# A feed-forward stage written out without loops: the down blocks of one token tile between the gate/up units of the next

## The reference

```
x = x + cross_attention(layernorm(x), ctx_2048)            # 512 wide, output projection wo
x = x + causal_attention(layernorm(x))                     # 16 heads of 128, rope, biases
x = x + ffn(layernorm(x))
ffn(x): gate, up = x @ W_gu.T   (W_gu: 2816 x 512, fp4 codes times a scale per 128 inputs)
        h = silu(gate) * up     (1408 wide)
        y = h @ W_down.T        (W_down: 512 x 1408, fp4 codes times scales)
        return y / sqrt(mean(y*y) + 1e-6)
```

## Time and profile before

| | us |
|---|---|
| median of 3 runs | 1392.92 (1392.2 to 1392.96) |
| the profiled execution, its own time | 1399.19 |
| span of its instructions | 1397.4 |
| TensorE busy in the span | 1344.6 |
| VectorE busy | 1006.3 |
| ScalarE busy | 507.1 |
| GpSimd busy | 375.9 |

### The profile page before, as it was taken

The page is one execution under the profiler, slowest core; times in us unless marked ns, Lnnn a source line. Parts: engine busy times, 40 slices in busy tenths (PEclk is TensorE's granted clock), DMA queues, the critical chain, the costliest instruction groups (busy, mean ns, idle before and its releaser), DMA issues. The chain is left out here.

```text
span 1397.4 us, 24040 instructions
## 1 busy us (share of the span) xinstructions
PE 1344.6 (96%) x9220; PEld 776.4 (56%) x9220; DVE 1006.3 (72%) x2309; ACT 507.1 (36%) x1249; POOL 375.9 (27%) x302
## 2 busy tenths in 40 slices
PE   8999999967999999999999999999899999999998
PEld 6666666534666666666666666654344434343433
DVE  6444444247888888888888887838899696969693
ACT  3222222222343333433343334320001665748281
POOL 0000000003222222222222222203033482919192
PEclk9999999989999999999999999999999999999999
DMA  8555555522101111111201021376841000000000
GB/s 333 211 197 199 202 192 189 214 83 87 31 31 31 44 45 50 31 31 61 61 31 31 16 61 31 91 190 193 187 162 61 1 1 30 0 30 0 30 1 30
DMA packets 36927, 122.47 MB, mean 88 GB/s; under 512 B 4313, under 2 KB 4953, under 8 KB 28121
## 3 DMA queue, kind: packets, MB, share of 16 engines
q1 hardware_dynamic: 36552, 118.19, 25.4%
q10 hardware_dynamic: 272, 2.88, 0.9%
HBM read 95.89 MB, written 25.17 MB: 87 GB/s over the span
## 5 line engine op out<-in xcount | busy, mean ns | idle before, releaser
L871 POOL TENSOR_TENSOR hd_rotated<-hd_products 64x512 f32<-64x512 f32 x32 | 40.3, 1259 | 741.0 <-DVE hd_products L1123 741.0
L191 PE MATMUL psum<-hd_xt_hi,hqk_hi 128*128 128x512 f16 x512 | 194.6, 380 | 1.6 <-DVE hd_xt_lo L1097 1.6
L192 PE MATMUL psum<-hd_xt_lo,hqk_hi 128*128 128x512 f16 x512 | 194.3, 379 | 0.0
L193 PE MATMUL psum<-hd_xt_hi,hqk_lo 128*128 128x512 f16 x512 | 194.3, 379 | 0.0
L1480 POOL TENSOR_TENSOR ff_part<-ff_part 128x512 f32<-128x512 f32 x88 | 127.8, 1468 | 103.9 <-DVE ff_part L1607 103.5
L191 PE MATMUL psum<-hd_wv_hi,hd_xt_hi 128*128 128x256 f16 x512 | 140.3, 274 | 4.2 <-DVE hd_wv_lo L1102 4.2
L1509 PE MATMUL psum<-ff_xt_hi,gu 128*128 128x512 f16 x352 | 133.9, 380 | 9.0 <-DVE w_rows L1645 3.3
L192 PE MATMUL psum<-hd_wv_lo,hd_xt_hi 128*128 128x256 f16 x512 | 140.4, 274 | 0.0
L193 PE MATMUL psum<-hd_wv_hi,hd_xt_lo 128*128 128x256 f16 x512 | 140.3, 274 | 0.0
L1510 PE MATMUL psum<-ff_xt_lo,gu 128*128 128x512 f16 x352 | 133.4, 379 | 0.0
L1607 DVE SCALAR_TENSOR_TENSOR ff_part<-psum,gu_scale,ff_part 128x512 f32<-128x512 f32 x176 | 119.8, 738 | 6.3 <-ACT ff_part L1557 3.6
(11 more groups left out here) (181 smaller groups left out, 3007.1 us busy)
## 6 DMA issues: line engine op xcount, KB each, us to landing
xa_kv_t<-in_ctx_t_dram SPq DMA_DIRECT2D x16, 1024.0 KB, 5.7
xa_kv<-in_ctx_dram SPq DMA_DIRECT2D x16, 1024.0 KB, 4.8
w_rows<-in_head_weights_dram SPq DMA_DIRECT2D x12, 1024.0 KB, 8.0
z_scratch<-hd_z_hi SPq DMA_DIRECT2D x32, 256.0 KB, 2.6
z_scratch<-hd_z_lo SPq DMA_DIRECT2D x32, 256.0 KB, 3.3
w_rows<-z_scratch SPq DMA_DIRECT2D x8, 1024.0 KB, 8.9
hqk_lo<-z_scratch SPq DMA_DIRECT2D x8, 1024.0 KB, 8.4
xn<-in_x_dram SPq DMA_DIRECT2D x8, 512.0 KB, 3.9
```

What stands on the lines that cost most here:

```text
L191: pe.matmul(out, lh, rh, start=(first and i == 0), stop=False)
L192: pe.matmul(out, lh, rl, start=False, stop=False)
L193: last = pe.matmul(out, ll, rh, start=False, stop=(final and i == k - 1))
```

## The change

The feed-forward phase is written out for all tiles. For tile 0 the 22 units run as before on eight banks. Then, for each t of 0 to 2, TensorE takes three down jobs of tile t, the transposes of tile t+1, six more jobs, and then the 22 units of tile t+1, with the other 35 jobs spread behind them: `beside` cuts the 35 jobs in 44 pieces, two pieces behind each whole unit (about 1.6 jobs). The last tile's 44 jobs run alone at the end. Groups and transposes use six banks in turn (6, 7, 0, 1, 2, 3), down products banks 4 and 5. ScalarE, after squaring, also copies the down product out of its bank into `results`, in all tiles but the last; the last step `finish` on VectorE then reads it from there. `h_hi`, `h_lo` and `results` are doubled. VectorE's layernorm is cut in pieces (`side_work`) put behind units: in tile 0 only the four `scale_block`s of tile 1, since the statistics of tile 1 are taken in `merge_phase` after add 13; in tiles 1 and 2 two block statistics behind units 0 and 2, small steps behind 4 and 6, `scale_block` behind 8, 10, 12, 14. In tiles 2 and 3 the roots of tile t-2 are behind units 5 and 7 and `finish` behind 9, 11, 13, 15. `second_halves` of the next tile come before the last `gated`. The four small transposes are gone, and the first unit waits for each `xt_lo` part alone. In `merge_phase` the load of `x1` of tile 1 moves from `heads_phase` to behind the codes of group 1, that of tile 3 to behind the next `z` load.

```diff
...
                 sp.dma_start(early.codes, codes_of(gu_codes, 0)).then_inc(early_sems.codes_loaded, 16)
-                for t in range(2):
-                    sp.dma_start(early.x2[:, t * TT:(t + 1) * TT, :], rows_of(t * TILE)).then_inc(early_sems.x1_loaded, 16)
+                sp.dma_start(early.x2[:, 0:TT, :], rows_of(0)).then_inc(early_sems.x1_loaded, 16)
...
-        x1_loaded, x1_ready = {t: sem(f"x1_{t}_loaded") for t in range(2, NT)}, sem("x1_ready")
+        x1_loaded, x1_ready = {t: sem(f"x1_{t}_loaded") for t in range(1, NT)}, sem("x1_ready")
...
+            load_x1(1)
             for t in range(1, NT - 1):
                 sp.wait_ge(z_used[1], t)
                 load_z(t, 1)
                 if t == 2:
+                    load_x1(3)
                     load_down()
                 if t == NT - 2:
                     sp.wait_ge(z_stored, 16 * (HEADS_SMALL + 2 * NT * PAIRS))
...
                 load_z(t + 1, 0)
                 if t == 1:
                     load_x1(2)
-                    load_x1(3)
...
-                    pool.wait_ge(early_sems.x1_loaded, 32)
-                if b % TT == 0 and b >= 2 * TT:
+                    pool.wait_ge(early_sems.x1_loaded, 16)
+                if b % TT == 0 and b >= TT:
...
+                if b == NT * TT - 3:
+                    dve.wait_ge(added, 2 * TT)
+                    layernorm(dve, 1, x2[:, TT:2 * TT, :], xn, stat, ln_step, xn_ready, parts=(1, 2, 3, 4))
...
+        FIRST, SECOND = 3, 9
+        jobs = [(0, b) for b in range(SECOND)] + [(1, b) for b in range(3)] + [(0, b) for b in range(SECOND, FB)] + \
+            [(1, b) for b in range(3, FB)] + [(i, b) for i in (2, 3) for b in range(FB)]
+        beside = [jobs[SECOND:][n * (len(jobs) - SECOND) // (2 * UNITS):(n + 1) * (len(jobs) - SECOND) // (2 * UNITS)] for n in range(2 * UNITS)]
+        def unit_after(i):
+            return next(n for n in range(2 * UNITS) if (i, FB - 1) in beside[n]) // 2
+        ROUND, RESULTS = (6, 7, 0, 1, 2, 3), (4, 5)
+        tile_0 = [("x", 0, k) for k in range(KD)] + [("p", 0, u, g) for u in range(UNITS) for g in range(KD)]
+        in_order = []
+        for t in range(1, NT):
+            in_order += [("x", t, k) for k in range(KD)] + [("p", t, u, g) for u in range(UNITS) for g in range(KD)]
+        placed = [(unit, n % 8) for n, unit in enumerate(tile_0)] + [(unit, ROUND[n % len(ROUND)]) for n, unit in enumerate(in_order)]
+        placed += [(("y", t, i), RESULTS[i % 2]) for t in range(NT - 1) for i in range(TT)]
+        placed += [(("y", NT - 1, i), bank) for i, bank in enumerate((4, 6, 7, 0))]
+        banks = Banks(nc, ctx, "ff", placed, [])
...
+            for t in range(NT - 1):
+                sp.wait_ge(finished, TT * (t + 1))
+                store(t, 0, TT)
...
+            def gate_up(t, u, g):
+                first = u % 2 * FF + u // 2 * P
+                unit = ("p", t, u, g)
+                if u == 0:
+                    banks.wait_moved(pe, None, ("x", t, g))
+                banks.wait_room(pe, None, unit)
+                pe.matmul(psum_of(unit), gu[:, g, first:first + P], xt_hi[:, g, :], start=True, stop=False)
+                banks.fills(pe.matmul(psum_of(unit), gu[:, g, first:first + P], xt_lo[:, g, :], start=False, stop=True), None, unit)
+            def down(t, i, b):
+                unit = ("y", t, i)
+                h_hi, h_lo = h_pairs[t % 2]
+                if b == 0:
+                    banks.wait_room(pe, None, unit)
+                if i == 0:
+                    pe.wait_ge(h_lo_done, t * FB + b + 1)
+                last = three_passes(pe, psum_of(unit), [(h_hi[:, b, block_of(i)], h_lo[:, b, block_of(i)])],
+                                    [(down_hi[:, b, :], down_lo[:, b, :])], first=(b == 0), final=(b == FB - 1))
+                if b == FB - 1:
+                    banks.fills(last, None, unit)
+            turn_xn(0)
+            for u in range(UNITS):
+                for g in range(KD):
+                    gate_up(0, u, g)
+            for t in range(NT - 1):
+                for i, b in jobs[0:FIRST]:
+                    down(t, i, b)
+                turn_xn(t + 1)
+                for i, b in jobs[FIRST:SECOND]:
+                    down(t, i, b)
                 for u in range(UNITS):
...
                     for g in range(KD):
...
+                        gate_up(t + 1, u, g)
+                    for i, b in beside[2 * u] + beside[2 * u + 1]:
+                        down(t, i, b)
+            for i, b in jobs:
+                down(NT - 1, i, b)
...
+            def square(t, i):
+                unit = ("y", t, i)
                 banks.wait_filled(act, None, unit)
...
+                if t * TT + i:
+                    act.wait_ge(squares_done, t * TT + i)
+                act.activation(junk[:, :], psum_of(unit), ACT.Square, accum_out=squares[:, t % 2, i:i + 1]).then_inc(squares_done, 1)
+                if t < NT - 1:
+                    if t >= 2:
+                        act.wait_ge(out_stored[t % 2], 16)
+                    banks.moves(act.activation(results[t % 2][:, i, :], psum_of(unit), ACT.Copy), None, unit)
...
+                        hidden_hi(t, b - 2)
+                    if b == FB and t < NT - 1:
+                        first_halves(t + 1)
+                    for i in range(TT - 1):
+                        if t and unit_after(i) in (2 * b - 1, 2 * b):
+                            square(t - 1, i)
+                if t:
+                    square(t - 1, TT - 1)
+            for i in range(TT):
+                square(NT - 1, i)
...
+                dve.tensor_scalar(to, from_, stat["meanvar"][:, i, 0:1], stat["y"][:, i:i + 1], ALU.subtract, ALU.mult).then_inc(xn_ready, 1)
...
+            def root_start(t, first, end):
+                at = slice(first, end)
+                dve.wait_ge(squares_done, t * TT + end)
+                done(dve.tensor_scalar(rms["var"][:, at], squares[:, t % 2, at], 1.0 / D, RMS_EPS, ALU.mult, ALU.add))
+                inverse_root(dve, {k: v[:, at] for k, v in rms.items()}, done, rounds=1)
+            def root_end(first, end):
+                inverse_root(dve, {k: v[:, first:end] for k, v in rms.items()}, done, seed=False, rounds=2)
+            def finish(t, i):
+                to = results[t % 2][:, i, :]
+                from_ = to
+                if t < NT - 1:
+                    banks.wait_moved(dve, None, ("y", t, i))
+                else:
+                    dve.wait_ge(out_stored[t % 2], 16)
+                    from_ = psum_of(("y", t, i))
+                dve.scalar_tensor_tensor(to, from_, rms["y"][:, i:i + 1], x2[:, t * TT + i, :], ALU.mult, ALU.add).then_inc(finished, 1)
+            def side_work(t, u):
+                if t == 0:
+                    if u in (4, 8, 12, 16):
+                        scale_block(1, u // 4 - 1)
+                    return
+                if t < NT - 1:
+                    if u in (0, 2, 4, 6):
+                        statistics(t + 1, (u // 2 + 1,))
+                    if u in (8, 10, 12, 14):
+                        scale_block(t + 1, u // 2 - 4)
+                if t >= 2:
+                    if u == 5:
+                        root_start(t - 2, 0, TT)
+                    if u == 7:
+                        root_end(0, TT)
+                    if u in (9, 11, 13, 15):
+                        finish(t - 2, (u - 9) // 2)
+            second_halves(0)
+            for t in range(NT):
                 for b in range(FB + 1):
...
+                    for u in (2 * b, 2 * b + 1) if b < FB else ():
+                        scale_and_add(t, u)
+                        side_work(t, u)
+                    if b == FB and t < NT - 1:
+                        second_halves(t + 1)
                     if b:
...
+                        gated(t, b - 1)
+            for t, first, end in ((NT - 2, 0, TT), (NT - 1, 0, 2), (NT - 1, 2, 3), (NT - 1, 3, 4)):
+                root_start(t, first, end)
+                root_end(first, end)
+                for i in range(first, end):
+                    finish(t, i)
...
         flat = hqk_lo[:, :, :].rearrange("p a n -> p (a n)")
...
+        h_pairs = (halves_in(flat, flat[:, FB * TILE:]), halves_in(*(w[:, :, :].rearrange("p a n -> p (a n)") for w in (wo_hi, wo_lo))))
+        results = tuple(w_rows[:, i, :].rearrange("p (b d) -> p b d", d=D) for i in range(2))
+        ffn_phase(nc, psum, ident, early.x2, xn, stat, gu, gu_scale, down_hi, down_lo, h_pairs, results, out.rearrange("b s d -> (b s) d"))
```

More of the change, by code:

```diff
@@ L1525, in tile @@
-                for blocks in (range(FB - 2), range(FB - 2, FB)):
-                    down(0, blocks)
-                    down(1, blocks)
-                for i in range(2, TT):
-                    if i == TT - 1 and not last_tile:
-                        turn_xn(t, t + 1)
-                    down(i, range(FB))
-            with nc.tensor.Fori(0, NT - 1) as t:
-                tile(t, False)
-            tile(NT - 1, True)
```

(32 more changed lines are left out.)

205 lines of the change are left out of this document (71 added, 134 removed).

## The result

| | before | after |
|---|---|---|
| median of five runs, us | 1392.96 (1392.2 to 1394.24) | 1384.74 (1380.16 to 1388.15) |
| ratio | | 0.9921, interval 0.9892 to 0.9951 |
| profiled execution, its own time, us | 1399.19 | 1385.5 |
| span, us | 1397.4 | 1383.7 |
| first transposes of the feed-forward phase to the end, us | 303.2 | 291.0 |

A forecast was written before the change was run, and what follows sets the result against it. The feed-forward phase was taken as bound in turn by VectorE with GpSimd, and by TensorE. Gains of 1.9 (start) and 21.1 us (stalls), less 9.1 kept or new, net 13.9: 1392.9 to 1379.0, range 1372.0 to 1387.0.

The forecast's parts named there:

- the forecast case: Whole kernel: median between 1374.5 and 1384 us, chance 0.58.
- Start: Start of the feed-forward phase: first matmul 1.9 us earlier, waits for the next low halves give 0.5 back.
- Units of tile 0: Tile 0's 22 units: 4.3 us of stall kept, scale blocks half hidden; 2.9 if hidden fully, 5.7 in the open.
- Passages: Between tiles: jobs and transposes cover hidden block 8 and low halves; 0.8 us for three passages and the last stretch.
- Tiles 1 and 3: Units of these tiles: VectorE's side work stalls TensorE 0.5 us at most in tile 1, nothing in tile 3.
- Tile 2: First four blocks of tile 2: VectorE 27.0 us against TensorE's 22.0, banks worth some 2; 3.0 us of stall.
- The last step from SBUF and ScalarE's copies: `finish` with both inputs in SBUF takes 1.1 us (bounds 0.68 and 1.47); ScalarE's twelve copies are hidden by TensorE.
- Merge phase: Statistics of tile 1 hidden in VectorE's waits; moved `x1` loads worth 0, between 1.0 us gained and 1.5 lost.
- the step from the span to the median: Whole kernel: median of runs lies 6.3 us below the profiled execution, so 1385.3 profiled and 1379.0 median.
- the signs named: Profile after: last matmul near 1376.6, first gate/up 1096.3, tile 0 units 42 us, tile 2 waits, `gated` median 0.7 to 1.3.
- A: Tiles 1 to 3: VectorE bounds, small two-input steps wait 0.4 to 0.8 us each; 1382.5 to 1392, chance 0.20.
- B: Tiles 1 to 3: every small step waits a whole 1.28 us GpSimd instruction; slower than before, 1410, chance 0.04.

The follow-up runs named there:

- The short sum: Changed kernel with GpSimd's sum over 8 of 512 columns, output of no use: phase 281.0 us, median 1376.19.
- the early blocks: Changed kernel with tile 0's four scale blocks moved from behind units 4, 8, 12, 16 to behind units 0 to 3: phase 288.9 us, median 1382.48.
- The two runs on the loads: Changed kernel with the `x1` loads at their old places, median 1385.42 against 1385.33; kernel before with only those loads moved, ratio 0.9988.
- both moves: Changed kernel with roots and last steps of tiles 2 and 3 later and tile 0's scale blocks behind units 0 to 3: medians 1377.34 and 1378.92.
- the first group: Changed kernel run again, unedited, beside 17 runs of the kernel before: 1385.33 against 1396.66 us, ratio 0.9933 (0.9910 to 0.9957).
- the two where z came first: Changed kernel with roots, last steps and scale blocks moved, plus ScalarE's code loads of groups 2 and 3 waiting for z: medians 1379.05 and 1372.59.

## Why the prediction was right

The range, 1372 to 1387, holds the median of 1384.74; the forecast of 1379.0 is 5.7 us lower, and the median lies just above the forecast case (1374.5 to 1384). The sum was nearer in the profiled execution (1385.3 said, 1385.5 measured). Point by point:

*Start.* Said 1.9 gained and 0.5 given back. The first matmul is 2.0 us earlier after the transposes, and the next three groups come 0.15 us late each, 0.5 in sum. Right.

*Units of tile 0.* Said 4.3 us of stall, between 2.9 and 5.7. Measured from first matmul to first down job, 1094.78 to 1138.75, 44.0 us, less 38.0 and the 0.5 of the start: 5.5. **The term was mis-sized.** I had taken a scale block as 0.68 us, half hidden. Three of the four took 1.5 us, because they wait for GpSimd, each for a low half just begun. The short sum shows that GpSimd is the cause, the early blocks that the place matters.

*Passages.* Said 0.8 for all. The first down job follows at 0.22 us, and from it to the first unit of tile 1 are 7.6 us, which is 27 matmuls and the transposes. No stall, in any passage and at the end.

*Tiles 1 and 3.* Said 0.5 and nothing; measured 0.0 and 0.2.

*Tile 2.* Said 3.0 us, at units 4 to 7. Measured 64.2 against 59.1 between the first and the last matmul of its units, 5.1. The wait itself is 2.4 us and some 0.8 before it, at the place and from the cause that was named. What the sum lacked is the clock: in four of the five traces with this wait it fell to 1.2 GHz for a few us behind it. The phase of the changed kernel is 291.0 us with the fall and 289.3 without, where the same wait of 2.4 us left the clock at its full level, so it is worth 1.7 us. Without the fall the units of tile 2 take 62.6 us, 3.5 of stall where 3.0 was said. Waits for GpSimd in small steps are rarer and longer than my 0.22 each: most steps have 0.16 us and six between 1228 and 1243 have 1.1. Six times 0.95 is 5.7 us where I had 4.0. The four of them with two tensor inputs make 3.8, near what the sum had; the other two are the step L127 with one input, which the sum had as free. That is the same mistake as with the scale block.

*The last step from SBUF and ScalarE's copies.* Said 1.1 us and hidden. It takes 0.74, all twelve, although both inputs are in SBUF. Eight of the twelve have GpSimd at work near them; the last four run behind the units of tile 3, where GpSimd does nothing. The eight stand right behind a unit's adds, and so come before the sum that these adds release on GpSimd. That is not enough by itself, since the seven scale blocks that wait stand right behind adds too: they stand behind the first unit of a block, where GpSimd can still be in the low half of an earlier block, the eight behind the second, where in this kernel it is not. ScalarE's copies are hidden: tiles 1 and 3 run at TensorE's pace with them.

*Merge phase.* Said nothing, between 1.0 gained and 1.5 lost. The profiled executions differ by 2.9 us (154.8 and 151.9), and the phases before them by 1.4 the other way. That these nearly make up for what tiles 0 and 2 lost is luck. The two runs on the loads find no difference in the median.

*The step that failed* is the one from the span to the median: "The median of the runs lies 6.3 below the profiled execution", which I took to hold for both kernels. It was the place of one execution in a scatter of 17 us (1389 to 1406) that the first three runs (1392.2 to 1393.0) did not show: the changed kernel's profiled execution lies 0.8 above its median, and in the two traces of both moves it was the fastest of its runs. Against the 17 runs of before in the first group the change is worth 11 us by the medians and 9 by the ratio (6 to 13), which holds the 12.2 of the phase.

Two of the signs named did not come: `gated` has 0.68 in the median where 0.7 to 1.3 was said, and the units of tile 0 take 44 us and not 42.

The rivals: A, VectorE as the bound of whole tiles, and B, slower through GpSimd's instructions, had the right mechanism and the wrong size: tile 1 has nine small two-input steps and no stall. The Trainium skill, page "SBUF — State Buffer", section "Who interferes with whom", names beside instructions with two SBUF inputs also `tensor_scalar`, in a mode that takes both ports and only when its operands meet the conditions for it, as one that can contend with GpSimd, and says that the order of issue decides who waits. The trace agrees that a `tensor_scalar` waits, L1658 with its 1.44 us and L127 with 1.12. Whether they ran in that mode no run here shows; alone, L1658 takes 0.74 us, as long as the two-input last step. That either engine can be the one that waits is seen in `gated` and the sum; that it is the order of issue, the starts of the two executions neither show nor exclude. I had drawn only the page's first half into the sum.

## What to carry to other kernels

Where VectorE and GpSimd work beside each other, allow for each VectorE instruction on SBUF tensors, with one input or two, that it may have to wait for GpSimd's instruction and not only run its own length: a step on four columns can cost 1.1 us, and six of the 25 small steps in tile 2 did. Look at where GpSimd is at that moment. Side work right behind the instruction that releases GpSimd's next one went unhindered where GpSimd was idle or nearly done, and waited 71 times where GpSimd had begun something else, in ten traces. Two chains of side work behind the same few units held TensorE up; moving side work brought 5.3 and 2.1 us of the phase here without taking away an instruction. And before a profiled execution is set against a median, ask how far executions scatter and in which phase: the phase that was changed agreed to 0.1 us, or 1.7 by the clock, where the whole did to 17.

## What the runs showed that I had not expected

- A stall of TensorE of 2.4 us was followed by half clock in four of five traces, and not in the fifth, at the same place of the same phase. In the merge phase the clock did not fall behind the waits for z of 2.5, 2.8 and 2.8 us (three traces), and fell behind those of 3.1 to 12.4 us (nine). What decides was not looked into. Window of that fifth (the changed kernel with the loads back), to be set beside the row with 0.60 above:

```profile
1246.10:1250.40 4.30, 4.16 (x19) 1.77 (x20) 4.30 (x8) 3.15 (x8) 3.14 (x2) 1.00 0.00 0
```

- A one-input `tensor_scalar` of 128x512 in float32 with a strided view, 0.74 us alone, waits for GpSimd like one with two inputs. So does an int32 `tensor_scalar` of 128x4, 0.17 us alone and 1.12 beside GpSimd.
- Which of the two engines waits can differ between executions: 1.77 or 0.68 us for the same `gated`.
- The wait for z in the merge phase was 2.5 to 12.4 us long in eleven traces where the code loads could run beside z, was put off to near 1005 us in one, and was not there in the two where z came first. What else scatters before the merge phase, whose start lies between 937.4 and 943.8 us, was not looked into.
